# Conv weights by multiply-adds, half of the 7x7 products on ScalarE, sums and residual by other engines

## The reference

```python
# layer 0, channels last
xc = xc + window_attention(layernorm(xc))        # windows of 8x8, 8 heads
xc = xc + gelu(layernorm(xc) @ w_mlp1 + b1) @ w_mlp2 + b2
# layer 1, on x in NCHW
residual = x
h = einsum('bchw,oc->bohw', x, pw1_w) + pw1_b
gap = h.mean(axis=(2, 3))
scores = sigmoid(relu(gap @ fc1_w.T + fc1_b) @ fc2_w.T + fc2_b)
mask = 1 for the 32 best scores of each image, else 0
h = relu(h)
offsets = tanh(h.mean(axis=(2, 3)) @ off_w.T + off_b).reshape(B, 3, 2)
sel = (h * mask)[:, :32]
for i, (ksz, base) in enumerate([(3, dw3), (5, dw5), (7, dw7)]):
    w = base[:32] * (1 + sigmoid(offsets[:, i, 0])) + tanh(offsets[:, i, 1])
    y_i = depthwise_conv(sel, w)                  # same padding, ksz x ksz
out = einsum('bchw,oc->bohw', concat(y_0, y_1, y_2), pw_w[:, :96]) + pw_b + residual
```

## Time and profile before

| | us |
|---|---|
| median of 3 runs | 327.58 (324.09 to 327.97) |
| profiled execution, its time | 323.53 |
| profiled execution, span from first to last instruction | 321.7 |
| busy: PE, DVE, ACT, POOL | 272.8, 243.6, 208.6, 126.8 |
| mean granted TensorE clock | 0.948 |
| tail, from the last attention matmul's neighbourhood to the end | 185 to 321.7 |

### The profile page before, as it was taken

The page is one execution under the profiler, slowest core; times in us unless marked ns, Lnnn a source line. Parts: engine busy times, 40 slices in busy tenths (PEclk is TensorE's granted clock), DMA queues, the critical chain, the costliest instruction groups (busy, mean ns, idle before and its releaser), DMA issues. The chain is left out here.

```text
span 321.7 us, 6621 instructions
## 1 busy us (share of the span) xinstructions
PE 272.8 (85%) x2474; PEld 214.3 (67%) x2474; DVE 243.6 (76%) x471; ACT 208.6 (65%) x339; POOL 126.8 (39%) x174
## 2 busy tenths in 40 slices
PE   1657878999999999999987996996888999499993
PEld 1335665867777676777766663553588889499993
DVE  2776448388787878978883558798899999999933
ACT  6686733959586685957546969857260773887731
POOL 5052536667676786765635404252250000000000
PEclk9987989999999999999999899996999799779998
DMA  7971374433343353335320000831238368377851
GB/s 173 202 156 34 82 169 114 100 93 85 78 110 83 80 111 74 82 75 115 87 64 2 0 0 4 170 78 34 76 61 179 85 125 174 87 157 149 173 108 33
DMA packets 35118, 31.06 MB, mean 97 GB/s; under 512 B 20816, under 2 KB 30032, under 8 KB 35088
## 3 DMA queue, kind: packets, MB, share of 16 engines
q1 hardware_dynamic: 30608, 23.55, 31.6%
q0 software_dynamic: 3392, 6.17, 11.0%
q10 hardware_dynamic: 1088, 0.94, 1.3%
HBM read 4.54 MB, written 2.10 MB: 21 GB/s over the span
## 5 line engine op out<-in xcount | busy, mean ns | idle before, releaser
L1206 PE MATMUL psum<-shifted,conv_w 128*128 128x286 f32 x528 | 75.9, 306 | 5.4 <-ACT conv_w L823 5.4
L1206 PEld LDWEIGHTS psum<-shifted,conv_w 128*128 128x128 f32 x528 | 74.1, 199 | 7.0 <-issue 5.3
L975 PE MATMUL psum<-q_heads,k_blocks 128*128 128x256 f32 x384 | 63.1, 303 | 2.9 <-ACT probs L681 2.2
L975 PEld LDWEIGHTS psum<-q_heads,k_blocks 128*128 128x128 f32 x384 | 52.2, 193 | 13.9 <-ACT probs L681 6.3
L1356 DVE TENSOR_REDUCE maxima<-psum 128x8 f32<-128x512 f32 x64 | 40.5, 680 | 8.9 <-PE psum L949 8.9
L681 ACT ACTIVATE probs<-psum 128x512 f32<-128x512 f32 x64 | 37.6, 606 | 10.3 <-PE psum L975 9.3
L535 POOL DMA_DIRECT2D k_blocks<-k_parts x56 | 32.2, 582 | 8.3 <-PE psum L975 8.3
L896 PE MATMUL psum<-parts,center_average 128*128 128x512 f32 x64 | 23.5, 451 | 11.5 <-DVE parts L318 8.0
L318 POOL TENSOR_TENSOR parts<-square_logvar,parts 128x512 fp32r<-128x512 f32 x14 | 20.0, 1428 | 28.3 <-ACT square_logvar L694 17.8
L949 PE MATMUL psum<-k_heads,q_blocks 128*128 128x256 f32 x128 | 24.6, 313 | 7.4 <-DMA k_heads<-k_parts 6.9
L318 POOL TENSOR_TENSOR parts<-x,parts 128x256 fp32r<-128x256 f32 (+1 forms) x21 | 19.3, 931 | 27.3 <-ACT parts L630 20.2
(11 more groups left out here) (146 smaller groups left out, 487.3 us busy)
## 6 DMA issues: line engine op xcount, KB each, us to landing
shifted<-images SPq DMA_DIRECT2D x32, 243.8 KB, 4.6
q_heads<-q_parts SPq DMA_DIRECT2D x128, 32.0 KB, 2.2
k_blocks<-k_parts POOLq DMA_DIRECT2D x56, 64.0 KB
k_heads<-k_parts SPq DMA_DIRECT2D x64, 32.0 KB, 2.2
out<-x SPq DMA_DIRECT2D x8, 256.0 KB, 3.0
q_blocks<-q_parts POOLq DMA_DIRECT2D x28, 64.0 KB, 2.4
conv_w<-conv_w SPq DMA_DIRECT2D x10, 176.0 KB, 2.9
x<-in_x SPq DMA_DIRECT2D x6, 256.0 KB, 4.9
```

The lines of the kernel that those rows point to most:

```text
L975: ins = pe.matmul(bank[:, hh * G // 2:(hh + 1) * G // 2], k_blocks[:, hh, w // (NW // 2), k_part, w % (NW // 2), :], q_heads[:, w // (NW / ...
L1206: ins = pe.matmul(psum[:, CONV[bh][g], 0:SPAN], conv_w[bh][:, w_part, h * NSLOT + slot, :], shifted[:, bh, part, stream, first:first + SPA ...
```

## The change

In words, part by part:

- **Products.** Of the 7x7 kernel's 14 tiles VectorE makes the seven of half 0 in one instruction. ScalarE makes the seven of half 1, each as a copy of `fuse_w` scaled by one tap (a scale read from memory). Unit u+1's seven stand between `odd_high(u)` and `odd_low(u)`.
- **Multiply-adds.** The 5x5 and 3x3 kernels' products and additions (four instructions) become sixteen multiply-adds of 64 columns each, ten and then six, with the tap as a scalar read from memory. They wait for `ac_product`.
- **Shared group.** `keep_shared` is one instruction on 128 partitions, and `result` first adds it to the two other groups in PSUM, then to x2. `add_shared` goes. The addition waits for `pe_conv`.
- **Means.** `h_sum` goes. `add_mlp` writes the sum of x2 beside its result (`x_sum`), and two small matmuls on TensorE, `gate_sums(k)`, make the mean of h of it ahead of `gate_means(k)`.
- **Order.** `gelu(3)` and `relu(1)` stand ahead of the last square-root work of the layer norm, `mlp2(3)` and `mlp2(7)` earlier (`mlp2(7)` in another bank), the banks of h alternate otherwise, and the gates' small steps move between these. ScalarE's loop over the last four units is written out.

The core of the diff:

```diff
+        def pointwise_bank(n):
+            return PW1[0] if n == 0 or n % 2 else PW1[1]
+        def mlp_bank(n):
+            return MLP if n < NG - 1 else HIDDEN0 + 2
...
+            def products(u, b4, bh, k):
+                act.wait_ge(S["gate_dve"], (k + 1) * GATE_STEPS)
+                if not (isinstance(u, int) and u < 2):
+                    act.wait_ge(S["low_weights"], u - 1)
+                for slot in range(TAP):
+                    ins = act.activation(whole_w[:, bh, 1, slot, :], fuse_w[:, 2, :], ACT.Copy, scale=tap_w[:, 2, bass.ds(2 * b4 + bh, 1), TAP + slot])
+                ins.then_inc(S["ac_product"], 1)
...
-                mine = shared[bh * C:(bh + 1) * C, :].rearrange("p (y v k) -> p y v k", v=2, k=W // 2)
-                for parity in range(2):
-                    r = slice(parity * C, (parity + 1) * C)
-                    ins = act.activation(mine[:, :, parity, :], sub_rows(psum[r, CONV[bh][0], :]), ACT.Identity, bias=vec[r, 10:11])
-                ins.then_inc(S["ac_shared"], 1)
+                act.activation(shared[:, bh, 0:SPAN], psum[:, CONV[bh][0], 0:SPAN], ACT.Identity, bias=vec[:, 10:11]
+                               ).then_inc(S["ac_shared"], 1)
...
-            with act.Fori(2, NB4) as b4:
-                for bh in range(2):
-                    keep_shared(2 * b4 + bh - 2, bh)
-                    high_weights(2 * b4 + bh, bh)
+            for u in range(4, 2 * NB4):
+                even_high(u, u % 2)
+                odd_high(u, u % 2)
+                if u + 1 < 2 * NB4:
+                    products(u + 1, (u + 1) // 2, 1 - u % 2, 2)
+                odd_low(u, u % 2)
+                if u + 1 < 2 * NB4:
+                    keep_shared(u - 1, 1 - u % 2)
...
+            def gate_sums(k):
+                b0, nb = GATES[k]
+                pe.wait_ge(S["dv_x2"], 2 * (b0 + nb))
+                if k == 0:
+                    pe.wait_ge(S["dv_whole2"], NG)
+                else:
+                    pe.wait_ge(S["gate_dve"], (k - 1) * GATE_STEPS + 14)
+                for half in range(2):
+                    ins = pe.matmul(psum[:, GATE, MEANS:MEANS + nb], pw1_w, x_sum[:, 2 * b0 + half:2 * (b0 + nb):2], start=half == 0, stop=half == 1)
+                ins.then_inc(S["pe_sums"], 1)
...
-                dve.scalar_tensor_tensor(mine, psum[:, MLP, :], vec[:, 8:9], mine, ALU.add, ALU.add).then_inc(S["dv_x2"], 1)
+                dve.scalar_tensor_tensor(mine, psum[:, mlp_bank(n), :], vec[:, 8:9], mine, ALU.add, ALU.add, x_sum[:, n:n + 1]).then_inc(S["dv_x2"], 1)
...
-                dve.tensor_reduce(h_sum[:, bass.ds(n, 1)], psum[:, PW1[half], :], AX.X, ALU.add).then_inc(S["dv_hsum"], 1)
...
-                dve.tensor_tensor(taps_window(whole_w[:, bh], 2), *factors(b4, bh, 2), ALU.mult)
-                dve.tensor_tensor(product5[:], *factors(b4, bh, 1), ALU.mult)
-                dve.tensor_tensor(product3[:], *factors(b4, bh, 0), ALU.mult).then_inc(S["dv_product"], 1)
+                dve.tensor_tensor(whole_w[:, bh, 0, 0:TAP, :], *factors(b4, bh), ALU.mult).then_inc(S["dv_product"], 1)
...
+                dve.wait_ge(S["ac_product"], u + 1)
+                for step, m in enumerate((1, 0)):
+                    dve.wait_ge(S["dv_product"], 4 * u + 1 + step)
+                    for h in range(NKT // TAP):
+                        for slot in range(TAP - KERNELS[m], TAP):
+                            tile = w[:, h, slot, :]
+                            tap = tap_w[:, m, bass.ds(2 * b4 + bh, 1), h * TAP + slot]
+                            ins = dve.scalar_tensor_tensor(tile, fuse_w[:, m, :], tap, tile, ALU.mult, ALU.add)
+                    ins.then_inc(S["dv_product"], 1)
...
+                dve.tensor_tensor(made, made, rows(shared[:, bh:bh + 1, :]).to_broadcast([128, 2, H // 2, W // 2]), ALU.add
+                                  ).then_inc(S["dv_shared"], 1)
```

More of the change, by code:

```diff
@@ L856, in _ @@
             relu(0, 0, 0)
+            gelu(3, 1)
+            relu(1, 0, 1)
             load_tables(LN_AND_EXP)
@@ L859, in _ @@
             load_tables(GELU)
-            relu(1, 0, 1)
-            gelu(3, 1)
             gelu(4, 0)
@@ L868, in _ @@
             relu(4, 2, 0)
+            products(0, 0, 0, 0)
+            gelu(7, 1)
+            products(1, 0, 1, 0)
             even_high(0, 0)
-            gelu(7, 1)
             odd_high(0, 0, range(1))
@@ L877, in _ @@
             relu(7, 3, 1)
+            products(2, 1, 0, 1)
             keep_shared(0, 0)
[L879 removed]
+            even_high(2, 0)
+            odd_high(2, 0)
+            products(3, 1, 1, 1)
+            odd_low(2, 0)
             gate(2)
             keep_shared(1, 1)
[L882 to L886 removed]
+            even_high(3, 1)
+            odd_high(3, 1)
+            products(4, 2, 0, 2)
+            odd_low(3, 1)
+            keep_shared(2, 0)
+            for u in range(4, 2 * NB4):
[6 more added lines that the diff above has]
+                    keep_shared(u - 1, 1 - u % 2)
             keep_shared(2 * NB4 - 2, 0)
@@ L1177, in _ @@
             mlp1(4)
+            mlp2(3, 1)
+            gate_sums(0)
+            pointwise1(2, 0)
             gate_means(0)
-            pointwise1(2, 0)
+            mlp1(5, range(0, 2))
             gate_scores(0)
-            mlp2(3, 1)
-            mlp1(5, range(0, 2))
-            gate_spread(0)
             mlp1(5, range(2, 4))
             pointwise1(3, 1)
+            gate_spread(0)
             mlp2(4, 0)
@@ L1243, in _ @@
             passes(0, 0, 1)
[L1244 removed]
             pointwise1(7, 1)
             passes(0, 0, 2)
+            gate_spread(1)
             low_passes(0, 0)
```

123 lines of the change are left out of this document (52 added, 71 removed).

## The result

The changed kernel took 336.77 us (median of 4 runs, 335.87 to 337.71) against 326.91 (median of 4, 324.09 to 327.97) for the kernel before. The ratio is 1.034, with a 95% interval from 1.029 to 1.039: slower by over 2%. Its profiled execution took 336.54 us with a span of 334.7; that of the kernel before took 323.53 with 321.7.

A forecast was written before the change was run, and what follows sets the result against it. VectorE was taken to set the rhythm, TensorE just behind. Terms -1.0 (to unit 2), +1.9, +0.4, +5.7 (units 4 to 7), -0.8 (end) made +6.2: 329.7 us profiled, 333.8 as median; range 325 to 341.

The forecast's parts named there:

- the loop: Units 4 to 7: each unit's cycle grows from 9.0 to 10.9 us, +5.7 us over three units.
- The closed cycle: One unit's casts, next unit's ScalarE copies, VectorE's multiply-adds and last weight steps wait on each other in turn: 10.9 us.
- Units 2 to 4: Unit 2 to 3 takes 10.9 instead of 9.0 us, +1.9; unit 3 to 4, with the gates' chain between, +0.4.
- On VectorE alone the rewriting is worth nothing: VectorE's weights of a unit: sixteen multiply-adds replace removed products and additions, 4.85 us against 4.9.
- To unit 2's weights: -1.0: Stage before unit 2's weights: removed reads outweigh two new waits and delays, cast at 249 against 249.85, -5 to +3.
- the clock's price: TensorE's lower clock after idling, expected to show only in the last unit's matmuls: 0 to +1.7 us.
- Unit 0 behind relu(4): Unit 0's seven ScalarE copies stand behind relu(4), so its weights are whole at 220.8 against 218.75: +2.0 us.
- Of the MLP order I make nothing: The reordered MLP steps ahead of the convolution: same work, ScalarE ending it at the same time, so no effect.
- the net -4.2: VectorE ahead of unit 2's weights: eight reads and three tiny reductions removed, eight sums written, net -4.2 us.
- The result of a unit and the end: The PSUM addition takes 0.72 us and hides in VectorE's wait except at the end, which shortens by 0.8 us.
- Rival 1: Short instructions are cheap: cycle 9.3 us, just under TensorE's 9.4, opening keeps its gain; -6, 321.5 us; chance 0.17.
- Rival 2: Loop as forecast, but the opening, before unit 2's weights, gives back 4 to 5 us: +2.5, 330 us; chance 0.25.
- Rival 3: The multiply-adds run at half rate, 1.1 us a unit over eight units: +15, 342.5 us; chance 0.08.

The follow-up runs named there:

- e5: The kernel before with only the sixteen multiply-adds in place of the four product and addition instructions; VectorE still makes all 14 tiles: 328.97 us, 1.014.
- e1: The changed kernel with ScalarE's seven copies of unit u+1 ahead of even_high(u), for units 5 to 7 only: 328.53 us.
- e3: The changed kernel with TensorE's gate_sums(2) ahead of unit 1's matmuls instead of behind 28 of them: 334.52 us.
- e4: The changed kernel with both moves, copies of units 5 to 7 ahead of even_high and gate_sums(2) ahead of unit 1's matmuls: 325.75 us.
- e2: The changed kernel with all 14 tiles of the 7x7 kernel made by VectorE and no copies on ScalarE: 331.23 us.
- e7: The kernel before with only the h_sum reads replaced by sums from add_mlp and TensorE's gate_sums, gate_sums(2) ahead of unit 1's matmuls: 326.47 us, 1.002.
- e8: The kernel before with both the PSUM addition and the sums by TensorE, without multiply-adds, ScalarE copies or the MLP order: 327.12 us, 1.010.
- e9: The changed kernel with the old products and additions, no ScalarE copies, and gate_sums(2) ahead of unit 1's matmuls: 320.76 us, 0.982 to the kernel before.
- e11: Size probe on the changed kernel: six multiply-adds of 128 elements for twelve of the sixteen, the other four tiles left out: 322.29 us (one run).

## Why the prediction was right in its sign, and where it failed

The forecast was 333.8 us in a range of 325 to 341, and 336.8 came. By differences it was further off: +6.2 was forecast, +9.9 came by the medians and +13.0 between the two traces. Of the 6.8 us between forecast and trace, 5.4 are the opening, 1.3 the loop and 0.3 the stretch between; the end is 0.3 better.

**The loop: right, sized low.** The closed cycle is there, and its wait on the copies (2.5 us a unit predicted, 2.69 measured). By its terms: casts 4.94 (predicted 4.94), copies and handoff 1.82 (1.70), multiply-adds 3.38 (3.1), L1635 and L1638 1.19 (1.18), together 11.33 against 10.9. The mis-sized term is the distance of the multiply-adds, 0.185 forecast and 0.206 measured; it was worked out from the overlap of longer neighbours. The duration was met (0.27). The distance makes 0.3 of the 0.43 us a unit, the handoff behind the copies 0.12; over three units this is the 1.3 us by which 5.7 was short of 7.0. The copies were met: 0.24 apart, median 333 ns. TensorE's need of 9.4 us a unit, taken from the chain, was too high: at a granted clock of 1.00 unit 7's 66 matmuls took 9.01 us.

**Units 2 to 4: met, in part by luck.** From unit 2's cast to unit 3's it is +1.6 for +1.9, but from 11.04 to 12.60 us, and not from 9.0 to 10.9: before, that step was longer than the loop's. From unit 3's to unit 4's it is +1.1 for +0.4.

**"On VectorE alone the rewriting is worth nothing": nearly.** e5 put 0.7 us a unit on it, 0.5 of which is the half of L1582 that VectorE keeps there, and the rest the distance again.

**"To unit 2's weights: -1.0": this step failed.** It was +4.4, and 254.3 us lies beyond the 253 at which the text said it would be wrong. How far beyond depends on TensorE's clock: e1, alike up to here, had this cast at 251.55, +1.7 against before, within the text's limits but still 2.7 above the forecast. The wait ahead of `gate_means(2)` was foreseen, but as 2.8 us, and it was 4.9. TensorE got unit 1's weights late, at 240.86, since its making was delayed; it had then been idle 3.40 us, and its 28 matmuls took 6.68 us instead of the 3.9 that I took from a TensorE at work. Each of the two puts the sums some 3 us later, VectorE's own delay of 3.5 (243.07 against 239.5) takes part of it back: 2.8 + 2.9 + 2.8 - 3.5 = 5.0. e3 shows what it was worth: 5.0 us from the load to unit 2's cast, 3.2 where TensorE was faster (e4 against e1). I had applied the clock's price (of the earlier trace rows) to the end of the program, where it didn't come (unit 7's 66 matmuls), and not to this place, where TensorE had just idled. In the changed kernel the low clock came once more ahead of it (222 to 228 us, 0.72), and unit 1's making stood behind these matmuls: 1.4 us of its delay, by the comparison with e1.

The other part of unit 1's delay is GpSimd. Its sixteen multiply-adds took 4.89 us instead of 3.35: two of them took 0.81 us (from 230.0) and 1.28 (from 230.7) instead of 0.27. GpSimd's timeline of the changed kernel beside them:

```profile
229.91 0.79 POOL L597 TENSOR_TENSOR images<-pair_sums,images 128x256 fp32r<-128x256 f32 x1 [3.94 <-DVE images L1523]
230.66 1.25 POOL L595 TENSOR_TENSOR images<-square_logvar,images 128x512 fp32r<-128x512 f32 x1
```

It was the same 4.88 in e1, e3 and e4, with the same two instructions beside them. The prediction had this kind of delay once (about 1 us, from L1591 at 215.25), and sized it by that one row; 1.5 came. Against before it is hardly a loss: there unit 0's weights paid 1.4 us beside GpSimd (L1583 1.32 for 0.82, L1591 1.72 for 0.83), and in the changed kernel unit 0's paid nothing. The Trainium skill, "SBUF — State Buffer", section "SBUF: two separate sides", says that a VectorE instruction with two SBUF inputs and a GpSimd instruction that reads SBUF share a port pair, which the first to start holds for its whole instruction. The multiply-adds of 811 and 1285 ns beside GpSimd instructions of 0.79 and 1.25 us agree, but no run here took GpSimd's work away.

**Unit 0 behind relu(4): right in time, the cause not shown.** Its cast started at 220.5 (220.8 predicted). But VectorE waited only 0.69 us for the copies there, and e2, without that wait, had the cast no sooner: its first instruction is 0.5 us longer and its multiply-adds took 4.29 us, with GpSimd beside them.

**"Of the MLP order I make nothing": wrong,** though not in the sum of this kernel. e7 and e8 have VectorE's savings in the old order and lose them to waits on TensorE; e9 has the same work in the new order and takes 6.4 us less than e8. Without the new order the net -4.2 that I booked for the removed reads would not have been there at all, and in it e9's opening is 2.4 us shorter than before's. Much of the difference is TensorE's clock (5.1 us of slower matmuls in e8, none in e9). How much of it is the MLP's order, how much the gates' places and how much the banks, no run tells. The sums themselves were cheap, as booked: the instruction behind `add_mlp` that writes them out took 0.08 us.

**The result of a unit and the end: right.** L1655 took 0.70 us (0.72 predicted), the end -1.1 (-0.8).

**The rivals.** Rival 1 fell: without the memory scalar the cycle was still 10.38 us, well above 9.4. Rival 2 expected the opening to give back 4 to 5 us; it lost 4.4. Rival 3, the half rate, fell with e11 (332 ns where it wanted 400). The Trainium skill, "Vector Engine (DVE) Microarchitecture Reference", section "Points that are easy to get wrong", says that this shape with two fp32 inputs from SBUF runs at half rate; that is not borne out here, with 1.03 ns for each element between 64 and 128.
